# One 128x2048 DMA transpose an item in place of four of 128x512, and an expert's rows parted one step sooner

## What is computed

```
x = x + 0.5 * ffn(layernorm(x))
x = x + attention(layernorm(x))          # 16 heads of 16, causal, rotary
x = x + 0.5 * ffn(layernorm(x))          # x: 2 x 2048 x 256, f32

ffn(h):
  scores = softmax(h @ gate.T)           # 16 experts
  w, idx = top_k(scores.T, cap)          # each expert takes 256 tokens of each sequence
  out = shared expert on every token
  for each expert: out[idx] += w * (gelu(x_e @ Wg.T) * (x_e @ Wu.T)) @ Wd.T,  x_e = h[idx]
```

## Time and profile before

| | before |
|---|---|
| median of 3 runs | 1661.98 us |
| the profiled execution, device time | 1665.68 us |
| its span | 1663.7 us |
| busy PE / DVE / ACT / POOL | 1508.0 / 892.6 / 1089.6 / 565.9 us |
| granted TensorE clock, mean over the span | 0.965 |
| steps of experts, first feed-forward | 185 to 545 us |
| steps of experts, second feed-forward | 1307 to 1664 us |

### The profile page before, as it was taken

How to read it: one execution, slowest core, us unless ns; L and a number is a source line. 1 busy time by engine, 2 the same in 40 slices (tenths; PEclk the granted TensorE clock), 3 DMA queues, 4 the chain that set the end, 5 groups by cost and what they waited for, 6 DMA issues and landing times. The chain is left out here.

```text
span 1663.7 us, 26653 instructions
## 1 busy us (share of the span) xinstructions
PE 1508.0 (91%) x9845; PEld 1040.8 (63%) x9845; DVE 892.6 (54%) x1982; ACT 1089.6 (65%) x1395; POOL 565.9 (34%) x500
## 2 busy tenths in 40 slices
PE   6999888887879899999999999999999887888887
PEld 4888677676679684333343343346788676777676
DVE  7888555455554794132144142157888555555554
ACT  7222355555554689999999999998222355555552
POOL 5001435555434793121111111112000435455544
PEclk9999999999889999999999999999999999999998
DMA  8222456876664689524146245113222466767763
GB/s 275 75 72 69 129 135 144 153 151 137 136 139 82 204 264 241 112 46 79 33 94 120 59 84 79 52 39 127 79 68 73 124 141 150 142 153 154 139 142 38
DMA packets 187443, 196.79 MB, mean 118 GB/s; under 512 B 84337, under 2 KB 149361, under 8 KB 184561
## 3 DMA queue, kind: packets, MB, share of 16 engines
q1 hardware_dynamic: 159136, 147.36, 34.5%
q0 software_dynamic: 28176, 47.73, 16.8%
HBM read 123.73 MB, written 55.57 MB: 108 GB/s over the span
## 5 line engine op out<-in xcount | busy, mean ns | idle before, releaser
L2482 ACT ACTIVATE 6390_pr<-6390_pS 128x1024 f32<-128x1024 f32 x448 | 420.6, 1191 | 2.9 <-PE 6390_pS L2374 2.9
L2405 PE MATMUL 6390_pO<-6390_pr,6375_vres 128*32 128x512 f32 x1792 | 238.1, 605 | 0.7 <-ACT 6390_pr L2482 0.7
L351 PE MATMUL 6401_pGU<-columns_ahead,weights_wts 128*128 128x512 f32 (+1 forms) x400 | 165.3, 413 | 57.9 <-DVE weights_wts L755 32.0
L351 PE MATMUL 93_pGU<-columns_ahead,weights_wts 128*128 128x512 f32 (+1 forms) x368 | 153.0, 416 | 56.6 <-DVE weights_wts L755 33.2
L2374 PEld LDWEIGHTS 6390_pS<-sq_rows,sk_rows 50*128 50x128 f32 x896 | 77.5, 184 | 179.7 <-ACT 6390_pr L2482 131.9
L2374 PE MATMUL 6390_pS<-sq_rows,sk_rows 50*128 50x512 f32 x896 | 183.9, 469 | 2.3 <-issue 1.3
L1096 ACT ACTIVATE hidden_hT<-6401_hf 128x512 fp32r<-128x512 f32 (+1 forms) x100 | 61.5, 615 | 170.0 <-DVE 6401_hf L1274 168.5
L1096 ACT ACTIVATE hidden_hT<-93_hf 128x512 fp32r<-128x512 f32 x96 | 60.7, 632 | 165.6 <-DVE 93_hf L1274 163.4
L1546 POOL DMA_INDIRECT out<-eo,6401_idx x64 | 107.4, 1678 | 151.8 <-issue 115.2
L352 PE MATMUL 6401_pGU<-columns_ahead,weights_wts 128*128 128x512 f32 (+1 forms) x400 | 158.9, 397 | 0.0
L353 PE MATMUL 6401_pGU<-columns_ahead,weights_wts 128*128 128x512 f32 (+1 forms) x400 | 158.5, 396 | 0.0
(11 more groups left out here) (441 smaller groups left out, 3724.1 us busy)
## 6 DMA issues: line engine op xcount, KB each, us to landing
93_raw_g<-WgT SPq DMA_DIRECT2D x16, 512.0 KB, 5.5
93_raw_u<-WuT SPq DMA_DIRECT2D x16, 512.0 KB
93_raw_d<-WdT SPq DMA_DIRECT2D x16, 512.0 KB
q_rows<-rows_halves SPq DMA_DIRECT2D x8, 1024.0 KB, 5.4
k_rows<-rows_halves SPq DMA_DIRECT2D x8, 1024.0 KB, 5.1
6401_raw_g<-WgT SPq DMA_DIRECT2D x16, 512.0 KB, 5.1
6401_raw_u<-WuT SPq DMA_DIRECT2D x16, 512.0 KB
6401_raw_d<-WdT SPq DMA_DIRECT2D x16, 512.0 KB
```

The lines of the kernel that those rows point to most:

```text
L351: pe.matmul(out, w_hi, x_hi, start=start, stop=False)
L2405: m = t_.matmul(pO[e * 32:(e + 1) * 32, j % 2, off:off + wd], vres[:, (g // GB) * TPB + kt, at:at + 32], from_(e), start=n == first[j], st ...
L2482: s_exp.done(a.activation(to, pS[:, u % RING, :, :], ACT.Exp, scale=HD ** -0.5))
```

## The change

`part_planes(s + 1)` moves from the head of step s+1 to step s, right behind `join_planes(s)`. Only the first expert item but one, J + 1, is still parted at the head of its own step. `turn_planes` issues one DMA transpose of all four tiles (source 128 x 2048 u16) where it issued four of 128 x 512; the turned planes are laid out tile by tile, and the join reads them so, with as many elements as before. On SyncE the transpose of an item moves ahead: it stands between the loads of the up and the down weights instead of ahead of the gate weights of the following expert.

```diff
--- before.py
+++ after.py
@@ -486,7 +486,7 @@
             routing_at = region("routing", 10 * KB)
             rows = routing_at("rows", [P, 4, P], f32)
             planes = routing_at("planes", [P, 4, 2 * D], self.u16)
-            turned_planes = routing_at("turned_planes", [P, 2, DC, W], self.u16, 4 * KB)
+            turned_planes = routing_at("turned_planes", [P, 4, 2, DC, P], self.u16, 4 * KB)
             idx = t.sb("idx", [P, E, B, CAP // P], self.i32)
             st6, mv = t.sb("st6", [P, 2, 4, 6]), t.sb("mv", [P, 2, 4, 2])
             std, rstd, shift = (t.sb(n_, [P, 2, 4]) for n_ in ("std", "rstd", "shift"))
@@ -566,7 +566,7 @@
                 sig("dve_" + n_) for n_ in ("stats", "mv", "rstd", "shift", "xl", "soft", "rows", "mul", "hl", "ev", "wl", "wt",
                                             "dif", "cnt", "route", "go", "hot", "idx"))
             s_wls, s_whs = sig("pool_wl"), sig("pool_wh")
-            s_planes, s_planes_turned, s_joined = sig("planes"), sig("planes_turned", 64), sig("act_joined")
+            s_planes, s_planes_turned, s_joined = sig("planes"), sig("planes_turned", 16), sig("act_joined")
             lowered = lambda n: 2 * n - (4 if ready else 0)
             left = lambda q: q - 2 if ready and q < 5 else q - 1
             s_Dq, s_evq = sig("pe_last_D"), sig("dve_last_ev")
@@ -769,10 +769,8 @@
                 def turn_planes(item):
                     s_planes.wait(sp, item - J)
                     s_joined.wait(sp, DC * (item - J - 1))
-                    for q in range(4):
-                        s_planes_turned.part(sp.dma_start_transpose(
-                            turned_planes[:, :, :, q * P:(q + 1) * P].rearrange("p h c t -> p (h c) t"),
-                            planes[:, q, :]), 16)
+                    s_planes_turned.done(sp.dma_start_transpose(turned_planes[:, :, :, :, :].rearrange("p q h c t -> p (q h c) t"),
+                                                                planes[:, :, :].rearrange("p q w -> p (q w)")))
 
                 for q in range(J):
                     if q >= first and not ready:
@@ -805,11 +803,12 @@
                 load_residual(7)
                 load_weight(1, 1)
                 load_weight(1, 2)
+                turn_planes(J + 1)
                 for e in range(2, E):
-                    turn_planes(J + e - 1)
-                    for w in range(3):
-                        load_weight(e, w)
-                turn_planes(NI - 1)
+                    load_weight(e, 0)
+                    load_weight(e, 1)
+                    turn_planes(J + e)
+                    load_weight(e, 2)
                 if lead:
                     self.load_projection_weights(sp)
                     s_wl.wait(sp, 3 * E)
@@ -1063,8 +1062,8 @@
                     s_planes_turned.wait(a, n)
                     s_U.wait(a, 4 * (item - 1))
                     for c in range(DC):
-                        s_joined.done(a.activation(joined[:, col, c, :].bitcast(self.u16).rearrange("p (t h) -> p t h", h=2),
-                                                   turned_planes[:, :, c, :].rearrange("p h t -> p t h"), ACT.Copy))
+                        s_joined.done(a.activation(joined[:, col, c, :].bitcast(self.u16).rearrange("p (q t h) -> p q t h", t=P, h=2),
+                                                   turned_planes[:, :, :, c, :].rearrange("p q h t -> p q t h"), ACT.Copy))
                     s_joined.wait(a, DC * n)
                     s_xh.part(a.activation(XT[0][:, col, :, :], joined[:, col, :, :], ACT.Copy), DC)
 
@@ -1143,7 +1142,7 @@
                         continue
                     if s == J + 1:
                         gathered(J)
-                    if J < s < NI:
+                    if s == J + 1:
                         part_planes(s)
                     if J < s < NI - (2 if lead else 0):
                         split(s, 0)
@@ -1162,6 +1161,8 @@
                         split(J, s - J + 3)
                     if J < s < NI:
                         join_planes(s)
+                    if J < s < NI - 1:
+                        part_planes(s + 1)
                     if J < s < NI - (2 if lead else 0):
                         split(s, 2)
                     if lead and s == NI - 3:
```

## The result

The changed kernel takes 1551.93 us (median of four runs, 1550.99 to 1552.49) against 1662.6 us before (four runs). The ratio is 0.9334, 95% interval 0.9309 to 0.936: 111 us faster. The profiled execution has a span of 1549.3 us, 114.4 less than before.

What follows compares the result with a forecast made beforehand. A ring of waits through the transposes bounded the expert steps; afterwards the gather's ring would. 4 steps at 17.6 plus 22 at 18.7 give 481.8 against 564.8, 83 us less: 1579 us, range 1552 to 1618.

Steps and rivals of the forecast that it cites:

- ring two: Expert steps after the change: evacuation, scatter, gather to rows 18.2 us, then parting to evacuation 18.63; 36.8 per two steps, 18.4 each.
- the five stretches: Quiet step before the change, parting to next parting: 9.21 + 5.78 + 1.82 + 1.13 + 3.11 = 21.05 us.
- Ring one: Expert steps after the change, ScalarE and VectorE waiting on each other without any transfer: 17.57 us a step.
- The second half of the ring: From gathered rows through parting, down-weight split, rest of the step and join to the evacuation: 18.63 us.
- The allowance of 0.3 for crowded transfers: Half the transposes' 0.65 us excess over their quiet step, added to 18.4 for one gather per two steps: 18.7.
- The four first steps: First two steps of each feed-forward, rows gathered ahead of any scatter: 4 x 17.6 = 70.4 us.
- T = 8: One transpose takes 8 us from issue to landing, hidden up to 10.8; four to one is itself worth nothing.
- The end of the first feed-forward, set at 0: Last expert's late down weights lose 7 to 12 us once; waits that go offset it: 0, 3 either side.
- SyncE's queue: Up weights have about 7.8 us against a median landing of 5.5; later down weights cost nothing but in one place.
- the gather doesn't bind: Rival: rows landing 2 us sooner leave steps of 17.6, 24 us less, 1555 us; chance 0.1.
- Another limit comes in first: Rival: PE's clock or colliding transfers set about 19.8 us a step, 24 us more, 1603 us; chance 0.2.
- The slow stream: Rival: one transpose takes 17.6 us, making steps of 23.0 and 34 us more, 1696 us; chance 0.06.

## Why the prediction was right or wrong

The direction and the kind of limit were right, the size was not: forecast 83 us less, measured 111, and the median of 1551.93 lies just below the range, which began at 1552. The step that failed is the length of ring two, the gather's: 18.4 us a step, with 0.3 added for crowding, where the runs showed 17.75 in the quiet steps and 17.86 on the mean.

- **What bounded the kernel**: right. The sum of the five stretches gave 21.05, and cutting one stretch (one transpose alone) gave 19.27 where its parts give 19.28.
- **Ring one, 17.57**: right; 17.43 in the steps whose parting waits for nothing. The first step of each feed-forward is shorter, 16.07 and 16.16, since its join started late; the sum had 17.6 for it.
- **Ring two, the gather** (the step that failed): right in kind, and it decides in the changed kernel. Its size was too large. "I take 18.2 us from evacuation to rows" measured 1336.14 - 1319.21 = 16.93 and, in the next step, 1352.90 - 1336.69 = 16.21. In both the rows are there 1.8 to 1.9 us after the last gather's issue ends (1334.31 and 1351.03), where the trace of before had 3.1, beside 0.52 MB of SyncE's queue. Those bytes were not the transposes', whose join runs from 1425.54: they were the load of the gate weights, issued behind the transposes at 1423.51, 13.2 us after the evacuation. Now that load goes out 8.4 us after it (1327.62) and has landed when the last rows come; this, too, the change moved. That the rows come sooner for it fits both traces, but no run moved the load alone. In the next step POOL's scatters were also issued more quickly. The second half of the ring, 18.63, measured 35.49 - 16.93 = 18.56. So 35.49 / 2 = 17.75 a step.
- **The allowance of 0.3 for crowded transfers**: too large, 0.1 was seen (17.86 on the mean against 17.75). It was carried over from the transposes, which had been the ones that were late. The 22 steps forecast at 18.7 took 17.86, so 18.4 us less: about 14 by the leg from evacuation to rows (1.27 / 2 a step), 4 by the allowance. The four first steps took 67.1 where 70.4 was forecast, 3.3 us. So 481.8 forecast, 460.1 measured: 21.7 of the 28 us that the medians miss.
- **T = 8, "four to one is itself worth nothing"**: wrong as a statement on the edit, though hidden in the sum. T is 4.9 to 5.7 us where nothing is issued shortly ahead, and 5.6 to 7.8 half a us behind the up weights, by the run that does it twice; in the changed kernel both cases occur, and its T is hidden. Alone four to one gave 61 us; on top of the parting it is worth 5, mostly by the last expert's weights.
- **The end of the first feed-forward, set at 0**: the wait for `raw_d` came. The load went out 6.9 us after the join and the split began 10.99 after it (444.58 - 433.59), at the near edge of the forecast 11 to 16, so 6.75 later than before; 4.85 of that is idle. The wait for the last gate weights went, as forecast, and these two intervals between joins took 45.98 us against 49.07. With the start, the stretch up to the second feed-forward's first join and the end, 9.7 us were gained outside the 26 steps, of which the sum held none.
- **SyncE's queue**: the up weights never made ScalarE wait in the regular steps, as forecast. That the transpose's place had slack was my reading afterwards, and one load further back cost 15 us.
- **The rivals**: "the gather doesn't bind", 1555, was nearest in size, but the gather does bind, as the run with it moved shows (5 us less). Its premise, rows 2 us sooner, came out in the second of the two steps only (16.21 against 18.2). "Another limit comes in first" did not come in the change itself: no join waited, and PE's clock rose. The Trainium skill ("DMA: Bandwidth & Descriptors", section "Issuing engines are not separate DMA queues") has all transfers share the 16 DMA engines; the traces agree so far as the gather's last rows took 3.1 us beside SyncE's load and 1.8 without it. Right behind a third load of SyncE's own queue the transpose took 9.8 us against 4.9 to 5.7. The slow stream didn't come: one transpose is faster than four.
- **The range** let the gather's ring fall only to ring one everywhere, and counted nothing below that from the ends of the feed-forwards.

## What to carry over

Sum the ring of waits from start to start, and then sum the next ring too, with the stretches as they will be once the first is cut: a transfer's time that was read beside other traffic is an upper bound, not a value, where the change moves that traffic away, and what varied with one transfer gives no allowance for another. Two edits that cut the same ring are not worth their sum, so time each alone. When a ring of two engines stands just above PE's own matmul time, look for one instruction on it that nothing needs so soon; here one swap on VectorE gave 20 us.

## What was not expected of the hardware

One DMA transpose of 128 x 2048 u16 takes 1.9 to 4.0 us to issue in the changed kernel's steps. In the run that does it twice it takes 4.9 to 5.7 us from issue to landing with a load of 512 KB issued 1.3 us or more ahead, and 5.6 to 7.8 with one issued 0.5 us ahead; right behind the last of three loads it took 9.8. Four of 128 x 512 take 5.2 us to issue and 7.1 to 9.2 to land. And PE's share of busy time in these views is no proof of a bound: at 221.41 of 226.64 us busy it still had 0.8 us a step to give.
